# Three edits to the hand-overs between TensorE and its neighbours in a four-block transformer kernel: rows turned by chunks, a later wait, a causal mask by heads

## What is computed

```python
# 1: state-space mixer (32 heads, state 64, causal convolution of 4 taps), then a gated FFN
h = mixer(rmsnorm(x0, norm1_w), ...) + x0
out1 = h + silu(rmsnorm(h, norm2_w) @ gate_w.T) * (rmsnorm(h, norm2_w) @ up_w.T) @ down_w.T   # 1024 wide
# 2: low-rank experts, 2 of 8, rank 16
hw = einsum('th,erh->etr', x, A) * wmat.T[:, :, None]          # wmat: softmax of the best two logits x 16
out2 = x @ W.T + einsum('etr,eor->to', hw, B)
# 3: causal attention, 16 heads of 16
scores = where(causal, q @ k.T / 4, -inf);  out3 = softmax(scores) @ v @ Wo + bo
# 4: 64 experts, top 4, at most 32 tokens each, and two shared experts of 256
```

## Time and profile before

| what | value |
|---|---|
| time, median of 3 runs | 1105.45 us (1102.81 to 1106.56) |
| the profiled execution's own time | 1107.4 us |
| its span in the trace | 1105.7 us |
| mean granted TensorE clock | 0.985 of full |
| busy PE, PEld | 1013.1, 613.6 us |
| busy DVE, ACT, POOL | 782.9, 547.7, 394.3 us |

### The profile page before, as it was taken

How to read it: one execution, slowest core, us unless ns; L and a number is a source line. 1 busy time by engine, 2 the same in 40 slices (tenths; PEclk the granted TensorE clock), 3 DMA queues, 4 the chain that set the end, 5 groups by cost and what they waited for, 6 DMA issues and landing times.

```text
span 1105.7 us, 21370 instructions
## 1 busy us (share of the span) xinstructions
PE 1013.1 (92%) x7887; PEld 613.6 (55%) x7887; DVE 782.9 (71%) x1756; ACT 547.7 (50%) x1158; POOL 394.3 (36%) x605
## 2 busy tenths in 40 slices
PE   6999899999999998999999998989999998989766
PEld 3455546654555656754555666655455666657442
DVE  4888635678889755678889746678889636676526
ACT  4888621346888321446888311446888211431302
POOL 3566301132676011132666011132765101131652
PEclk9999999999999999999999999999999999999968
DMA  6899400003444000003444000004445704005657
GB/s 214 306 293 312 128 1 19 1 2 99 144 139 138 2 1 20 20 2 108 136 143 134 1 0 20 20 2 124 134 141 167 166 1 115 20 2 152 197 189 299
DMA packets 74743, 113.64 MB, mean 103 GB/s; under 512 B 6167, under 2 KB 64670, under 8 KB 73744
## 3 DMA queue, kind: packets, MB, share of 16 engines
q1 hardware_dynamic: 71952, 104.48, 30.5%
q0 software_dynamic: 1536, 3.60, 1.0%
q10 hardware_dynamic: 1152, 4.19, 0.9%
HBM read 93.46 MB, written 19.40 MB: 102 GB/s over the span
## 4 chain that ended last, share of the span: by engine, by line
PE 63%; DVE 14%; ACT 7%; issue 7%; POOL 5%; DMA 2%; SPq 0%; DVEq 0%; POOLq 0%; ACTq 0%
PE bank L970 25%; PE bank L1066 4%; PE bank L1157 3%; PE bank L1274 3%; PE bank L1320 3%; DVE hf L1876 3%; PE bank L1174 2%; PE bank L1364 2%; PE bank L1367 2%; PE bank L983 2%; DMA x<-cum_dram 2%; PE bank L961 2%; PE bank L1419 1%; PE bank L1081 1%; DVE hf L1890 1%
## 5 line engine op out<-in xcount | busy, mean ns | idle before, releaser
L970 PE MATMUL bank<-uT,w_in 128*128 128x512 f32 (+1 forms) x584 | 274.1, 608 | 6.8 <-DVE hf L1890 3.7
L1876 DVE SCALAR_TENSOR_TENSOR hf<-bank,conv_w,hf 128x510 f32<-128x510 f32 (+2 forms) x224 | 162.6, 743 | 34.6 <-ACT nmax L1550 20.0
L970 PEld LDWEIGHTS bank<-uT,w_in 128*128 128x128 f32 (+1 forms) x584 | 102.4, 188 | 126.8 <-issue 91.1
L1702 POOL TENSOR_TENSOR rs<-ve,half 128x2 f32<-128x2 f32 x56 | 38.9, 695 | 283.4 <-DVE ve L2028 283.3
L1533 ACT ACTIVATE hf<-bank,conv_b,conv_w 128x512 f32<-128x512 f32 x128 | 99.2, 775 | 53.8 <-PE bank L970 53.4
L970 PE MATMUL bank<-uT,w_gu 128*128 128x512 f32 x224 | 98.5, 593 | 0.0
L1157 PE MATMUL bank<-hf 64*64 64x128 f32 (+3 forms) x2048 | 88.1, 304 | 8.6 <-ACT x_pad L1577 3.5
L1157 PEld LDWEIGHTS bank<-hf 64*64 64x64 f32 x2048 | 74.0, 133 | 38.4 <-issue 30.7
L2325 DVE TENSOR_REDUCE nmax<-bank 128x2 f32<-128x256 f32 (+1 forms) x128 | 65.4, 553 | 20.4 <-PE bank L1367 18.2
L1511 ACT ACTIVATE xc<-bank 128x512 f32<-128x512 f32 x44 | 26.3, 597 | 104.1 <-PE bank L970 77.0
L970 PEld LDWEIGHTS bank<-uT,w_gu 128*128 128x128 f32 x224 | 42.4, 190 | 47.8 <-issue 47.3
(11 more groups left out here) (349 smaller groups left out, 2162.1 us busy)
## 6 DMA issues: line engine op xcount, KB each, us to landing
hf<-cum_dram SPq DMA_DIRECT2D x32, 384.0 KB, 3.5
dec<-cum_dram SPq DMA_DIRECT2D x32, 384.0 KB, 3.8
tmp<-cum_dram SPq DMA_DIRECT2D x32, 384.0 KB, 3.6
x<-cum_dram SPq DMA_DIRECT2D x32, 384.0 KB, 3.8
y_dram<-xf SPq DMA_DIRECT2D x16, 512.0 KB, 6.5
w_in<-in_w_in SPq DMA_DIRECT2D x1, 3584.0 KB, 11.4
w_in<-in_w_egu SPq DMA_DIRECT2D x6, 512.0 KB, 9.7
w_in<-y_dram ACTq DMA_DIRECT2D x5, 512.0 KB, 9.4
```

What stands on the lines that cost most here:

```text
L970: mm = pe.matmul(plan[key][0:n, :], w[:, k, cols], uT[:, k, :], start=k == 0, stop=k == DC - 1)
L1702: pool.tensor_tensor(rs[:, cols], ve[:, cols], half[:, cols], ALU.pow).then_inc(rstd_ready.sem, 1)
L1876: ins = dve.scalar_tensor_tensor(d, x, conv_w[:, j, TAPS - 1 - s:TAPS - s], d, ALU.mult, ALU.add)
```

## The change

Four things are done.

1. The transposes of the low-rank stage, and of the first half of attention, are split by channel chunk: chunk c goes to bank 4 + c, each with a semaphore of its own (`transposes_by_chunks`), and ACT copies 256 columns for each chunk (`turned_by_chunks`). The low-rank products and Q and K run the first chunk over all their results, then the second. The turned low-rank values (LT) are handed on by tile, no more by half.
2. The down products wait for the last two factors just before these are used by the first tile.
3. The mask of a step is laid down by eight matmuls of 64 columns in place of two of 256: for each quarter (part) of the 128 queries of a block and each of the two heads, 32 rows of weights on the head's own 32 partitions. `mask_rows` holds ones where the query comes before the part's key, `mask_keys` a diagonal of -1e30. These constants replace the identity in bf16 and qkey_mask.
4. ("T","moe",1) goes to bank 5 in place of bank 6, behind X of chunk 0, and PE waits for its copy ahead of the state products, which use bank 5 next.

The core of the diff:

```diff
-                plan.use(("T", "moe", 1), 6, r - 1)
+                plan.use(("T", "moe", 1), 5, r - 1)
             for w in range(2):
                 plan.use(("BC", 1, w), 6 + w, r)
...
                 plan.use(("F", j), 2 + j, r)
             for j in range(2):
-                plan.use(("T", "lora", j), 4 + j, r)
+                for c in range(DC):
+                    plan.use(("T", "lora", j, c), 4 + c, r)
             for t in range(TILES):
                 plan.use(("L", t), t, r)
-            for j in range(2):
-                plan.use(("LT", j), 4 + j, r)
+            for t in range(TILES):
+                plan.use(("LT", t), 4 + t % 2, r)
             if r == 0:
                 for n in range(3):
                     plan.use(("zeros_lora", n), 7, r)
-            plan.use(("T", "att", 0), 6, r)
+            for c in range(DC):
+                plan.use(("T", "att", 0, c), 4 + c, r)
             for c in range(DC):
                 plan.use(("Q", c, 0), 6 * c, r)
...
+        def transposes_by_chunks(pe, stage, n, src, j, r):
+
+            pe.wait_ge(u_ready.sem, u_ready.at(r, 2 * n - 1 + j))
+            for c in range(DC):
+                key = ("T", stage, j, c)
+                pe.wait_ge(*plan.before(key, r))
+                for i in range(2):
+                    mm = pe.transpose(plan.of(key, r)[:, i * P:(i + 1) * P],
+                                      src[:, 2 * j + i, c * P:(c + 1) * P], ident[:, :])
+                mm.then_inc(plan.fills(key, r), 1)
+
...
+        def of_key_part(bank, part):
+
+            both = bank[:, :].rearrange("p (b n) -> p b n", n=HKEYS)
+            return both[:, part:part + 2 * P // HKEYS + 1:2 * P // HKEYS, :]
 
...
+                if r > 0:
+                    pe.wait_ge(*plan.drained(("T", "moe", 1), r - 1))
 
                 def products(n):
...
                         linear(pe, ("G", f), w_gu, slice(f * P, (f + 1) * P), r)
                         linear(pe, ("U", f), w_gu, slice(FF + f * P, FF + (f + 1) * P), r)
-                for f in range(FF // P - 2, FF // P):
-                    pe.wait_ge(*plan.drained(("U", f), r))
                 for j in range(2):
                     pe.wait_ge(*plan.before(("F", j), r))
                     for i in range(2):
                         t = 2 * j + i
                         for f in range(FF // P):
+                            if t == 0 and f >= FF // P - 2:
+                                pe.wait_ge(*plan.drained(("U", f), r))
                             mm = pe.matmul(plan[("F", j)][:, i * D:(i + 1) * D], hf[:, f, t * P:(t + 1) * P],
                                            w_dn[:, f, :], start=f == 0, stop=f == FF // P - 1)
                     mm.then_inc(plan.fills(("F", j)), 1)
...
                     elif j == 1:
                         multiply_zeros(("zeros_lora", 0), 12, r)
-                    transposes(pe, "lora", 2, u, j, r)
-                    pe.wait_ge(*plan.drained(("T", "lora", j), r))
-                    for t in (2 * j, 2 * j + 1):
-                        pe.wait_ge(*plan.before(("L", t), r))
-                        for k in range(DC):
+                    transposes_by_chunks(pe, "lora", 2, u, j, r)
+                    for k in range(DC):
+                        pe.wait_ge(*plan.drained(("T", "lora", j, k), r))
+                        for t in (2 * j, 2 * j + 1):
+                            if k == 0:
+                                pe.wait_ge(*plan.before(("L", t), r))
                             mm = pe.matmul(plan[("L", t)][:, 0:LW], uT[:, k, t * P:(t + 1) * P],
                                            w_lora[:, k, :], start=k == 0, stop=k == DC - 1)
-                        mm.then_inc(plan.fills(("L", t)), 1)
+                            if k == DC - 1:
+                                mm.then_inc(plan.fills(("L", t)), 1)
                 for j in range(2):
                     pe.wait_ge(hw_ready.sem, hw_ready.at(r, j + 1))
-                    pe.wait_ge(*plan.before(("LT", j), r))
-                    for i in range(2):
-                        mm = pe.transpose(plan[("LT", j)][:, i * P:(i + 1) * P], hw[:, 2 * j + i, :], ident[:, :])
-                    mm.then_inc(plan.fills(("LT", j)), 1)
-                    pe.wait_ge(*plan.drained(("LT", j), r))
                     for t in (2 * j, 2 * j + 1):
+                        pe.wait_ge(*plan.before(("LT", t), r))
+                        pe.transpose(plan[("LT", t)][:, 0:P], hw[:, t, :], ident[:, :])\
+                            .then_inc(plan.fills(("LT", t)), 1)
+                    for t in (2 * j, 2 * j + 1):
+                        pe.wait_ge(*plan.drained(("LT", t), r))
                         pe.matmul(plan[("L", t)][:, 0:D], hwT[:, t * P:(t + 1) * P], w_lb[:, :],
                                   start=False, stop=True, skip_group_check=True).then_inc(lora_added.sem, 1)
                     if r == 0:
...
                     mm.then_inc(plan.fills(key), 1)
 
-                transposes(pe, "att", 3, u, 0, r)
-                pe.wait_ge(*plan.drained(("T", "att", 0), r))
-                for c in range(DC):
-                    for name in "QK":
-                        queries_or_keys(name, c, 0)
+                transposes_by_chunks(pe, "att", 3, u, 0, r)
+                for k in range(DC):
+                    pe.wait_ge(*plan.drained(("T", "att", 0, k), r))
+                    for c in range(DC):
+                        for name in "QK":
+                            key = (name, c, 0)
+                            if k == 0:
+                                pe.wait_ge(*plan.before(key, r))
+                            mm = pe.matmul(plan.of(key, r)[:, 0:HALF],
+                                           w_att[:, k, "QK".index(name), c * P:(c + 1) * P],
+                                           uT[:, k, 0:HALF], start=k == 0, stop=k == DC - 1)
+                            if k == DC - 1:
+                                mm.then_inc(plan.fills(key, r), 1)
...
                         S = pair_banks(("S", n))
                         pe.wait_ge(*plan.before(("S", n), r))
-                        for i in range(2):
-                            pe.matmul(on_diagonal(S[:, i, :]), ident_bf[:, :], qkey_mask[:, :], start=True,
-                                      stop=False, skip_group_check=True)
+                        for part in range(P // HKEYS):
+                            for i, (h, rows) in enumerate(heads):
+                                pe.matmul(of_key_part(S[:, i, :], part), mask_rows[rows, part, :],
+                                          mask_keys[rows, :].unsqueeze(1).broadcast_to([HKEYS, 2, HKEYS]),
+                                          start=part == 0, stop=False, skip_group_check=True)
                     if k is not None:
                         bt, ct, et, heads_t = of_pair(k)
                         ot = bt * SEQ
...
+            def turned_by_chunks(stage, j, r):
+                for c in range(DC):
+                    key = ("T", stage, j, c)
+                    act.wait_ge(*plan.full(key, r))
+                    act.activation(uT[:, c, j * HALF:(j + 1) * HALF], plan.of(key, r)[:, 0:HALF], ACT.Copy)\
+                        .then_inc(plan.drains(key, r), 1)
+
...
-                    act.wait_ge(*plan.full(("LT", j), r))
-                    act.activation(hwT[:, j * HALF:(j + 1) * HALF], plan[("LT", j)][:, 0:HALF],
-                                   ACT.Copy).then_inc(plan.drains(("LT", j)), 1)
+                    for t in (2 * j, 2 * j + 1):
+                        act.wait_ge(*plan.full(("LT", t), r))
+                        act.activation(hwT[:, t * P:(t + 1) * P], plan[("LT", t)][:, 0:P],
+                                       ACT.Copy).then_inc(plan.drains(("LT", t)), 1)
...
                 ahead_rmsnorm(0, j)
             dve.wait_ge(consts_in, 160)
-            dve.tensor_copy(ident_bf[:, :], ident[:, :])
-            dve.tensor_copy(qkey_mask[:, :], cstage[:, 1, 0:2 * P])
+            dve.tensor_copy(mask_rows[:, :, :].rearrange("p h q -> p (h q)"), cstage[:, 1, :])
+            dve.tensor_copy(mask_keys[:, :], cstage[:, 0, TRI - HKEYS:TRI])
             dve.tensor_copy(earlier[:, :], cstage[:, 0, TRI:512])
...
-        "qkey_mask": np.concatenate([low.T, low.T], 1),
+        "mask_rows": np.concatenate([(q < 32 * h + k % 32).astype(f) for h in range(4)], 1),
         "row_parts": rows.reshape(128, 3, 16),
-        "earlier": (k < q).astype(f),
+        "mask_keys_earlier": np.concatenate([np.where(np.arange(32)[None, :] == k % 32, -1e30, 0.0).astype(f),
+                                             (k < q).astype(f)], 1),
```

More of the change, by code:

```diff
@@ L33 @@
 KEYS = P // 2
+HKEYS = 32
 TRI = 3 * P
@@ L819, in _ @@
             for dst, name in ((ident[:, :], "ident"), (iota[:, :], "iota"), (parity[:, :], "parity"), (late_keys[:, :], "late_keys"),
-                              (cstage[:, 1, 0:2 * P], "qkey_mask"),
```

(8 more changed lines are left out.)

6 lines of the change are left out of this document (2 added, 4 removed).

## The result

| | before | after |
|---|---|---|
| median of five runs each | 1104.97 us (1102.81 to 1106.56) | 1095.95 us (1093.46 to 1097.56) |
| profiled execution's span | 1105.7 us | 1092.6 us |

The medians differ by 9.0 us of 1105. The ratio is 0.9921 with a 95% interval of 0.9901 to 0.9941, a gain between 6.5 and 10.9 us. The forecast was 1099.2, that is -6.3 us. The direction was right and the time lies in the range; by the medians the gain is 2.7 us larger than the sum said.

A forecast was written before the change was run, and what follows sets the result against it. Hand-overs on the chain of waits, mostly through PE, were taken to bound the kernel, not engine throughput. Terms -4.2 - 1.8 - 1.8 - 0.5 + 2.0 = -6.3 us gave 1099.2 us, range 1094.5 to 1105.0.

The forecast's parts named there:

- down products: Wait moved behind the first six factors: PE no longer loses 1.05 us a round before these products, -4.2 us.
- low-rank and attention rows by chunks: ACT's shorter first copy lets low-rank products and Q and K start 0.44 us earlier each round, -1.8 us each.
- mask: Mask to score 0.2 us instead of 0.32, but DVE or ACT hides all but one step a round: -0.5 us.
- border: Last turned rows wait for DVE's third tap on bank 5, projection +0.66 us at three round borders: +2.0 us.
- The cover of the later Q: ACT keeps the first Q and K by 451.45, PE needs them at its first mask at 452.24: covered by 0.8 us.
- the bound of -3.6: Gain bound for the mask: 36 uncovered steps, nine in each round, at -0.1 us a step.
- A: Small mask weight loads cost as much as large ones, 0.88 us for eight: +14.2 us, 1119.7, slower; chance 0.09.
- B: Longer PE idling at round borders drops the granted clock at three: -1.2 us, 1104.3, same; chance 0.12.
- the prediction's sign: Half-clock stretches appearing in rounds 1 to 3 would show the forecast wrong; no size given for the sign itself.
- C: A slack behind absorbs the delay of the projection at the round borders: -8.3 us, 1097.2; chance 0.13.
- D: Two copies and more semaphores give back the 0.44 us gains of the chunks: -2.7 us, 1102.8, same; chance 0.09.

The follow-up runs named there:

- the runs with four masks: Changed kernel with the mask laid down four times over in steps 0 to 2 (1100.23 us), 3 to 8 (1099.63 us, single execution) or 9 to 15 (1095.61 us).

## Why the prediction was right, and where its sum was off

| term | forecast | stretches of the trace of after | edit alone |
|---|---|---|---|
| down products | -4.2 | 4 x -1.06 = -4.2 | -5.5 (-7.7 to -3.3) |
| low-rank and attention rows by chunks | -3.6 | 8 x -0.43 = -3.4 | -4.2 (-5.6 to -2.9) |
| mask | -0.5 | 4 x (-0.98 + 0.10) = -3.5 | -2.4 (-4.0 to -1.0) |
| border | +2.0 | 0.76 + 0.64 + 0.65 = +2.0 | +0.7 (-0.7 to +2.0) |
| sum | -6.3 | -9.1 | measured together: -9.0 |

The sum of the stretches meets the medians more closely than the interval of 6.5 to 10.9 us can confirm.

**Down products:** right in size and in what is late next. The products start at 406.58 and the gating ends at 407.54, so five of the twelve passes were needed as cover.

**Rows by chunks:** right, 0.44 as worked out from a shorter copy and an earlier start. The cover of the later Q held: ACT ended the first K at 446.19 and PE's mask came at 447.17, 0.98 for the 0.8 that the prediction had.

**Mask:** this is the step that failed. Its price was right enough: 0.2 us was taken, 0.13 measured, with the 25 ns of the narrow bf16 rows as the better bound. What was wrong is the sentence that DVE's maxima "set the pace" in the first steps, so that only one step's gain was kept. The earlier trace rows showed an idle time of 0.15 before the maxima of step 3, and I took it for all nine steps. Even that row says otherwise: its 1.02 us are both maxima of the step together, not each, a step of PE took 1.18 there (from the mask at 458.51 to that at 459.69), and the bracket names PE's scores as what DVE waited for. Steps 0 to 2 are apart from each other, by transposes and by the products of V, and there DVE idles 0.33 to 0.64 us for PE; the runs with four masks show steps 0 to 2 wholly on PE's side, 3 and 4 covered, 5 to 8 in part, 9 to 15 covered. It is the changed kernel in which DVE sets the pace in step 3, since PE then runs steps 2 and 3 side by side. The nine steps gave 0.88 us a round, not 0.13, and the term was -3.5, next to the bound of -3.6 that the prediction had named and not taken.

Part of each step's gain is not in the matmuls. Where 128-row work comes first, as before the first mask, the 0.1 us gap that lay between mask and scores now lies ahead of the mask (+0.10 in round 1 with the mask alone); only between two steps of scores is it gone.

**Border:** right, as a loss. The tap ended at 507.74, PE's transposes started 0.14 later where 0.05 was assumed, so +0.75 at the projection; +0.65 reached the x rows. Undoing it gained 2.0 us by the stretches and 3.5 by the ratios.

**Rivals.** A (small loads at the price of large ones) is far off: eight took 0.13 us up to the scores, not 0.88. The Trainium skill, TensorE: Matmul & The Clock Gate, section LDWEIGHTS, would put the eight loads at an estimated 0.86 us; the measurement decides against using it for such loads in a row, two heads at a time. B (the clock) did happen, but it goes with no edit: a short stretch at half clock (the 1.2 GHz level) stands ahead of the last 90 us in seven of the thirteen traces, at 123, 200, 479, 724 and 728 us and three times where round 3's output projection starts, each worth 1.7 us for 3.4 us of it and 2.8 to 3.0 for 6.8. One of them, in round 3 at 995, stood already in the trace of before, so the prediction's sign, a stretch at half clock in rounds 1 to 3, could not tell the change from chance. Ahead of each PE had idled 0.65 to 1.97 us; the same idle times stand in the other traces without such a stretch, so which execution gets one stays open. C is not borne out by the stretches, for the delay reaches ACT's x rows at all three borders; the times of the border alone would not exclude it. D fell with the rows by chunks alone.

Not settled: why the mask alone measured 1.1 us less than its stretches and the border alone 1.3 less than its. The sum of the four alone is -11.4 for -9.0 together; the intervals of a single edit are 2.6 to 4.4 us wide, so this needs no cause. How much of the mask's gain is its shorter matmuls and how much the side-by-side start of steps 2 and 3, no run separates.

## What to carry to other kernels

Price a hand-over by the distance between two marks on the chain, an instruction of PE ahead of it and one behind it, and ask for each step of a loop separately which engine is waited for: a row that shows a short wait in one step says nothing of the step before it. Where a buffer is moved to another bank, ask whose drain it then waits for; here a bank whose last user had long been drained, and whose next user comes one product later, gained 5.3 us by the stretches and 3.9 by the ratios over the one chosen. And a small operand can do more than shorten its own matmuls: with masks of 32 rows two steps on different partitions ran side by side.

## What the runs showed of the hardware

Matmuls of 64 columns with 32 rows of bf16 weights, a new weight load for each, follow each other at 28 to 29 ns on one set of 32 rows (twelve more cost 0.34 us), and two sets go at the same time, so that twenty-four cost 0.35 us. The order in which the program lists the two sets made no difference (0.13 us either way), and a score on one set started ahead of a mask matmul on the other that stands before it in the program (448.13 and 448.15). Between 128-row and 32-row work PE loses about 0.1 us: in the kernel before between mask and scores, where two matmuls of 0.11 leave 0.10 of the 0.32; with the new mask ahead of the first mask, which starts 5.38 instead of 5.28 us behind Q and K. The Trainium skill, TensorEngine Tiling (Array Packing), section Key Properties, says that a change of the tiling mode drains TensorE; the gap agrees with it. After DVE's tap PE started 0.14 us later (507.74 to 507.88), after ACT's copies 0.04 to 0.05.
